# A recurrent FFN kernel: two scan subtractions on GpSimd, a rounding moved on ScalarE, and gate chunk 1 made in halves

## What is computed

```
xn = layernorm(x)
s = attn_block(xn)                      # dequantised, low-rank parts
def W(w, base):
    d = w - base
    return base + mean(abs(d)) * sign(d)
h = silu(xn @ W(w1, m1).T) * (xn @ W(w3, m3).T)
out = x + s * silu(h @ W(w2, m2).T)
```

## Time and profile before

| | us |
|---|---|
| median of 3 runs (545.56 to 548.17) | 547.8 |
| span of the profiled execution | 543.7 |
| TensorE busy | 521.9 |
| VectorE busy | 441.2 |
| ScalarE busy | 332.3 |
| GpSimd busy | 100.6 |

### The profile page before, as it was taken

One profiled execution on the slowest core, in us unless ns is written; L12 is line 12 of the kernel. 1 busy time (PEld: TensorE's weight loads), 2 busy tenths in 40 slices (PEclk: granted clock), 3 DMA queues, 4 the chain that ended last, 5 costly groups with the idle time before them and its releaser, 6 DMA issues.

```text
span 543.7 us, 6429 instructions
## 1 busy us (share of the span) xinstructions
PE 521.9 (96%) x2317; PEld 428.4 (79%) x2317; DVE 441.2 (81%) x511; ACT 332.3 (61%) x452; POOL 100.6 (19%) x109
## 2 busy tenths in 40 slices
PE   1899989999999999999999999999999999999997
PEld 1677778888888788888887788787888878888886
DVE  6999995978886988975798987998979888874446
ACT  2989868555744566446758846966876576455310
POOL 0311023102200220022003120400320031004590
PEclk9999999999999999999999999999999999999999
DMA  8999913223822393039147993863383377027503
GB/s 337 401 402 401 364 50 118 68 69 78 165 87 68 54 213 85 0 81 228 42 96 147 238 220 79 172 128 68 70 164 72 74 151 149 7 59 161 143 19 135
DMA packets 31759, 76.98 MB, mean 142 GB/s; under 512 B 3856, under 2 KB 7184, under 8 KB 31600
## 3 DMA queue, kind: packets, MB, share of 16 engines
q1 hardware_dynamic: 21648, 57.68, 34.2%
q0 software_dynamic: 9792, 18.88, 20.0%
q10 hardware_dynamic: 288, 0.02, 0.0%
HBM read 53.49 MB, written 2.10 MB: 102 GB/s over the span
## 4 chain that ended last, share of the span: by engine, by line
PE 72%; DVE 15%; issue 7%; ACT 4%; DMA 1%; DVEq 0%; SPq 0%; ACTq 0%; POOLq 0%
PE gate_pair L1514 21%; PE up_ps L1514 18%; PE down_pair L1553 16%; PE down_ps L1553 8%; DVE acc L1216 4%; PE side_ps L1578 2%; DVE h L1129 1%; PE down_pair L1471 1%; ACT ramp L797 1%; PE up_ps L1651 1%; PE down_pair L1651 1%; PE gate_pair L1651 1%; ACT y_part L746 1%; DMA xn<-in_x 1%; DVE up_ps L1124 1%
## 5 line engine op out<-in xcount | busy, mean ns | idle before, releaser
L1514 PE MATMUL gate_pair<-xT,gu 128*128 128x512 f32 x696 | 165.1, 390 | 1.3 <-DVE gu L1095 0.8
L1514 PEld LDWEIGHTS gate_pair<-xT,gu 128*128 128x128 f32 x696 | 130.4, 188 | 28.9 <-DVE gu L1095 1.2
L1514 PE MATMUL up_ps<-xT,gu 128*128 128x512 f32 x624 | 146.6, 390 | 1.2 <-DVE gu L1081 0.7
L1514 PEld LDWEIGHTS up_ps<-xT,gu 128*128 128x128 f32 x624 | 116.8, 188 | 26.6 <-DVE gu L1081 1.1
L603 POOL DMA_DIRECT2D y<-y_part x64 | 55.3, 875 | 336.8 <-ACT y_part L746 335.7
L1553 PE MATMUL down_pair<-h,dn 128*128 128x512 f32 x447 | 108.1, 391 | 0.8 <-DVE h L1129 0.6
L733 ACT ACTIVATE h<-up_ps 128x512 fp32r<-128x512 f32 x52 | 31.1, 599 | 114.1 <-DVE up_ps L1124 61.8
L1553 PEld LDWEIGHTS down_pair<-h,dn 128*128 128x128 f32 x447 | 83.5, 188 | 19.8 <-ACT y_part L746 1.1
L797 ACT ACTIVATE ramp<-codes,bend_bias 128x1536 f32<-128x1536 uint8 x56 | 88.2, 1580 | 0.0
L1216 DVE SCALAR_TENSOR_TENSOR acc<-ramp,acc 128x1536 f32<-128x1536 f32 x42 | 73.7, 1754 | 4.8 <-ACT ramp L797 4.2
L1553 PE MATMUL down_ps<-h,dn 128*128 128x512 f32 x216 | 53.6, 391 | 0.5 <-ACT y_part L746 0.5
(11 more groups left out here) (196 smaller groups left out, 567.3 us busy)
## 6 DMA issues: line engine op xcount, KB each, us to landing
y<-y_part POOLq DMA_DIRECT2D x64, 256.0 KB, 4.3
scale<-in_scales SPq DMA_DIRECT2D x28, 384.0 KB, 5.5
scan_w<-in_w SPq DMA_DIRECT2D x15, 512.0 KB, 11.3
base<-in_mean SPq DMA_DIRECT2D x10, 768.0 KB, 4.9
scan_mean<-in_mean SPq DMA_DIRECT2D x9, 512.0 KB, 10.7
silu_gate<-in_mean SPq DMA_DIRECT2D x6, 512.0 KB, 12.5
codes<-in_codes SPq DMA_DIRECT2D x14, 192.0 KB, 5.4
xn<-in_x SPq DMA_DIRECT2D x4, 512.0 KB, 4.9
```

The lines of the kernel that those rows point to most:

```text
L1514: last = nc.tensor.matmul(ps[:, :], w[:, w_part, hc * P:(hc + 1) * P], xT[:, x_part, hc, th * HALF:(th + 1) * HALF], start=(hc == 0 and w_ ...
```

## The change

Three things change. `POOL_SCAN` names scan tiles 0 and 1, so GpSimd subtracts them, ahead of `early_low`, and no longer waits there for VectorE's first two subtractions; VectorE drops them, and runs `normalise(4)` to `normalise(7)` and all eight `x_low` in one go. ScalarE rounds the mean of unit 0 (`early_high`) behind `x_high(3)`, and turns to scan tile 0 only behind `x_high(7)`. Gate chunk 1 is made, rounded and completed in two halves of 256 columns, with semaphores for the first half, and TensorE's first six matmuls of it need the first half alone.

```diff
-POOL_SCAN = []
+POOL_SCAN = [0, 1]
+SPLIT_UNIT = 1
...
+            def scan_subtract(k):
+                scan_loaded(pool, k)
+                nc.gpsimd.tensor_tensor(scan_w[:, k % SCAN_W, :], scan_w[:, k % SCAN_W, :], mean_tile(k),
+                                        ALU.subtract).then_inc(scan_diff_pool, 1)
+
             def early_low():
                 pool.wait_ge(gu_hi, 1)
-                pool.wait_ge(scan_diff, dve_tiles(1))
...
+            for k in POOL_SCAN:
+                scan_subtract(k)
             early_low()
             unit_subtract(0)
...
             x_high(2)
             x_high(3)
-            scan_signs(0)
+            early_high()
             x_high(4)
             x_high(5)
-            early_high()
             x_high(6)
             x_high(7)
+            scan_signs(0)
             scan_signs(1)
...
-            unit_high(1)
+            split_high(0)
+            split_high(1)
...
+            def split_make(half):
+                sl = slice(half * HID // 2, (half + 1) * HID // 2)
+                dve.wait_ge(unit_sign, SPLIT_UNIT + 1)
+                nc.vector.scalar_tensor_tensor(unit_base(SPLIT_UNIT)[:, sl], unit_raw(SPLIT_UNIT)[:, sl],
+                                               coeff[:, GATE:GATE + 1], unit_base(SPLIT_UNIT)[:, sl], ALU.mult, ALU.add
+                                               ).then_inc(half_made if half == 0 else unit_made, 1)
...
-            scan_subtract(0)
             for t in range(4, TT):
                 normalise(t)
-            scan_subtract(1)
-            for t in range(4):
-                x_low(t)
-            for t in range(4, TT):
+            for t in range(TT):
                 x_low(t)
...
-            unit_make(1)
+            split_make(0)
+            split_make(1)
+            split_low(0)
+            split_low(1)
             early_scale(0)
-            unit_low(1)
             early_add(0)
...
-                if kind == GATE or k < FIRST:
+                if k == SPLIT_UNIT and kind == GATE and th == 0:
+                    pe.wait_ge(half_lo, 1)
+                elif kind == GATE or k < FIRST:
                     pe.wait_ge(gu_lo, gu_count(k, kind))
...
                 for hc in range(HC):
+                    if hc == HC // 2 and k == SPLIT_UNIT and kind == GATE and th == 0:
+                        pe.wait_ge(gu_lo, gu_count(k, kind))
```

More of the change, by code:

```diff
@@ L305, in block_kernel @@
         unit_made = sem("unit_made")
+        half_made = sem("half_made")
+        half_hi = sem("half_hi")
+        half_lo = sem("half_lo")
         early_part = sem("early_part")
@@ L683, in unit_signs, with split_high @@
                 nc.scalar.activation(unit_raw(u), unit_raw(u), ACT.Sign).then_inc(unit_sign, 1)
+            def split_high(half):
+                sl = slice(half * HID // 2, (half + 1) * HID // 2)
+                if half == 0:
+                    act.wait_ge(half_made, 1)
+                else:
+                    act.wait_ge(unit_made, SPLIT_UNIT)
+                nc.scalar.activation(unit_split(SPLIT_UNIT)[:, HI, sl], unit_base(SPLIT_UNIT)[:, sl], ACT.Copy
+                                     ).then_inc(half_hi if half == 0 else gu_hi, 1)
             def unit_high(u):
@@ L1074, in unit_make, with split_low @@
                                                ALU.mult, ALU.add).then_inc(unit_made, 1)
+            def split_make(half):
+                sl = slice(half * HID // 2, (half + 1) * HID // 2)
+                dve.wait_ge(unit_sign, SPLIT_UNIT + 1)
+                nc.vector.scalar_tensor_tensor(unit_base(SPLIT_UNIT)[:, sl], unit_raw(SPLIT_UNIT)[:, sl],
+                                               coeff[:, GATE:GATE + 1], unit_base(SPLIT_UNIT)[:, sl], ALU.mult, ALU.add
+                                               ).then_inc(half_made if half == 0 else unit_made, 1)
+            def split_low(half):
+                sl = slice(half * HID // 2, (half + 1) * HID // 2)
+                if half == 0:
+                    dve.wait_ge(half_hi, 1)
+                else:
+                    dve.wait_ge(gu_hi, SPLIT_UNIT + 1)
+                nc.vector.tensor_tensor(unit_split(SPLIT_UNIT)[:, LO, sl], unit_base(SPLIT_UNIT)[:, sl],
+                                        unit_split(SPLIT_UNIT)[:, HI, sl].bitcast(f32), ALU.subtract
+                                        ).then_inc(half_lo if half == 0 else gu_lo, 1)
             def unit_low(u):
```

## The result

| | before | changed |
|---|---|---|
| median of 20 runs each, us | 547.78 | 548.97 |
| lowest and highest run, us | 545.39, 548.47 | 547.94, 549.40 |
| profiled span, us | 543.7 | 547.6 |
| GATE coefficient, UP coefficient, us | 30.34, 48.85 | 33.38, 52.77 |
| first DOWN matmul, us | 75.46 | 79.47 |

What follows compares the result with a forecast made beforehand. TensorE bounds the kernel from 75.46 us; earlier, waits on VectorE and ScalarE set the coefficients, and lost time is carried. Terms 2.8 + 0.6 + 0.15 - 0.3 = +3.3 us on the 547.8 median gave 551.1 us, range 548.0 to 552.4.

Steps and rivals of the forecast that it cites:

- GATE coefficient: End of the early stretch: scan tile 2 reaches ScalarE at 26.95 instead of 24.16 us, delaying this coefficient to 33.1, +2.8 us.
- The mechanism: Layer norm: VectorE's normalisation of tiles 2 and 3 stalls until GpSimd's 2.35 us subtractions end; tile 4 is 2.0 us late.
- VectorE keeps its turn: Rival, layer norm: VectorE runs tiles 2 and 3 in one go, GpSimd's second subtraction holds the inverse root; 551.5 us, chance 0.10.
- not slower: Rival, layer norm: GpSimd and VectorE don't stall, tile 4 comes 1.14 us early; 547.6 us, chance 0.14.
- only two-operand work stalls: Rival, layer norm: tiles 2 and 3 on time, one inverse-root step held, tile 4 1.0 us late; 550.3 us, chance 0.20.
- unit 4 beside the halves: Gate chunk 1: its new halves meet GpSimd's subtraction of unit 4 and stall about 0.95 us instead of 0.33, +0.6 us.
- four half operations: Gate chunk 1 on VectorE: four half operations in place of two whole ones cost two more starts, +0.15 us.
- TensorE no longer late at the UP total: UP total: TensorE, 0.33 us behind VectorE's sum before, now waits for VectorE, which swallows that lateness, -0.3 us.
- TensorE ahead of the UP total: Sign in the new profile: TensorE should idle before the UP total, arriving early and waiting for VectorE.
- the clock did not fall: Rival denied here: idling about 2 us at the GATE total drops TensorE to 1.2 GHz, +1.8 us on top; 552.9 us, chance 0.04.
- the no-stall case: Layer norm: the rival *not slower*, without stalls between GpSimd and VectorE; 547.6 us, chance 0.14; the range starts just above it.
- the first two rivals: Layer norm: *not slower*, 547.6 us, chance 0.14, and *only two-operand work stalls*, 550.3 us, chance 0.20.

## Why the prediction was right, and where it was not

**The mechanism held.** GpSimd's subtraction takes 2.34 us (forecast 2.35), starts when the data land, and VectorE's normalisation stands still beside it. The order of turns held too: tile 2, GpSimd's second, tile 3; with it *VectorE keeps its turn* falls. Tile 4 came at 17.30 (forecast 17.15), x tile 7 was rounded by 22.2 (21.8), scan tile 2 reached ScalarE at 27.22 (26.95), the GATE coefficient stood at 33.38 (33.1). The Trainium skill, "SBUF — State Buffer", section "Who interferes with whom", says that a tensor_scalar within SBUF may take the pair of ports that VectorE shares with GpSimd. The prediction found no row for that; 4.19 us for 0.97 is one, and 0.97 without GpSimd's part is its counterpart. The rivals *not slower* and *only two-operand work stalls* fall with it.

**The sum came near in its total, less so in its terms.** Between the two profiles the UP coefficient moved by 52.77 - 48.85 = 3.92 us:

| term | forecast | measured | from |
|---|---|---|---|
| GATE coefficient | +2.8 | +3.04 | 33.38 - 30.34; some 0.35 of it a late landing |
| unit 4 beside the halves | +0.6 | +0.72 | 1.05 less the 0.33 lost before |
| four half operations | +0.15 | +0.44 | below |
| TensorE no longer late at the UP total | -0.3 | -0.27 | 48.54 - 48.21 before, 52.35 - 52.29 after |
| sum | +3.3 | +3.93 | |

The third term is the one that was mis-sized, by some 0.3 us. With unit 4 out of the way, VectorE's two makes and two LO parts start 0.97 and 0.74 us apart (33.16, 34.13, 34.87), 1.71 in all; the whole ones cost 0.66 and 0.61 before (30.54 to 31.20 and 31.99 to 32.60), 1.27. Four halves cost 0.44 more, not 0.15. That the halves gain nothing was right.

**TensorE ahead of the UP total.** The prediction wanted idle time there and there is none to speak of: TensorE arrives as the sum is ready (52.29, total at 52.35). The idle time is at the GATE total, 1.57 us (forecast about 2), and the clock did not fall after it.

**The base was wrong.** The step that failed is "The profiled execution spans 543.7 us, 4.1 below the median of the runs, 547.8; I add the sum to both". What lies around the span is 1.8 us. The other 2.3 us were the distance from the lower group, to which the profile belongs, to the upper one, in which the median fell. The right base for a sum made in that profile is 543.7 + 1.8 = 545.5 us, and 545.5 + 3.3 = 548.8 is within 0.2 us of the result. That 548.97 lies in the stated range is luck in part: the low end, 548.0, was set by the no-stall case on the wrong base, and by the median alone the result would have spoken for something between the first two rivals (547.6 and 550.3 us). What speaks for the mechanism is the profile. The table of times before could have told: its three runs had one at 545.56, which fits 543.7 with 1.9 us around it, and a gap of 2.2 us to the next. So could: PEclk 1.00 was read as a full clock throughout, though 18.38 shows four transposes that speed up on the way.

**Why the medians differ by less than the profiles.** In the kernel before TensorE has no slack between early mean and GATE total (29.92, right behind the sum at 29.71 + 0.16), so a late grant costs the whole 1.84 us there, and with unit 4 beside the LO part 2.3 us at UP. In the changed kernel it waits 1.57 us at that place; the grant came at 22.40 us, after the early mean had begun at 21.76, and the wait covered it. A grant as late as that of the upper run would be covered as well, by an estimate from these rows: the early mean would take 7.44 us for 6.01, 1.43 more, and the wait is 1.57. Against the lower group the change costs 3.5 us, against the upper about 1.0 (548.97 against 545.46 and 547.93). That the late clock makes the upper group is shown by the matmuls added. That the wait hides it is not shown as directly, since no run forced a late grant on the changed kernel; it is read from the profile, and it fits that kernel's lack of an upper group and the run with ScalarE's order alone, where 0.85 us were added to the lower group and nothing to the upper one. The chances reflected this badly: 0.57 for slower by over 0.5%, where the measured +0.38% (0.27 to 0.48) lies within that bound.

## What to carry over

An engine that takes work over can stop the one it relieves. Before moving a subtraction to GpSimd, list what VectorE does beside it: in these runs work with one operand in PSUM (1.27 us for two LO parts) and absolute sums (1.21 us) took no longer beside it; two operands in SBUF (2.59 us for 1.22), or a normalisation within SBUF (4.19 us for 0.97), waited until GpSimd was through.
Compare a profile's span with the run that it was, not with the median, and look at the single runs for groups before adding a sum to a median.
Where TensorE starts with scattered small work and then meets a stretch without slack, matmuls that nobody needs can see to it that the full clock is there in time. It took matmuls in every gap, which gave 24 of 24 runs in one group; one burst of fourteen did not do it.

## What the runs showed that was not expected

The grant of the full clock came at 18.99 and 24.55 us in the two profiles of the kernel before, and at 19.08 (ScalarE's order alone), 25.06 (the halves alone) and 18.66 (without GpSimd's part) in kernels whose TensorE did nearly the same until then. Some 1.7 us of the 2.3 between the groups come from this alone, the rest from unit 4, beside whose subtraction the late coefficient then puts VectorE. In the run with the single burst, where unit 4 was subtracted only at 34.75 us in the profile, the two groups stand 1.8 us apart. The Trainium skill, "TensorE: Matmul & The Clock Gate", section "Part 1: The HAM clock gate", says that the lower clock is the default, that activity lifts it, and that what watches the activity doesn't begin anew with a kernel, so that the moment varies from run to run. The runs agree that it varies, here by six microseconds. Falls came after waits of different length: the clock fell at 23.82 us after a wait of 1.96 us before 22.80, at 32.27 after 1.68 us before 31.31, at 20.80 after 1.67 us before 19.41; 1.57 us before 32.96 in the changed kernel, and 1.65 before 32.54 in that with unit 4 later, were followed by no fall.
